# Shifting, norming and transposing a token-major residual stream in a six-layer attention and feed-forward kernel

## The reference, cut to what matters

```python
x = L0_attn_x                                  # (2, 1024, 128)
xn = layernorm(x)
s = recurrent_branch(xn)                       # projections, causal conv, gates, scan, projection
y = xn
for i in range(6):
    y = attn_layer(shift_tokens(y), Wqkv[i], q_scale[i], k_scale[i], Wo[i]) + y    # 16 heads of 64, window 32
    y = ffn_layer(shift_tokens(y), ln_g[i], ln_b[i], W1[i], b1[i], W2[i], b2[i]) + y
out = x + s * silu(y)

def shift_tokens(t):                           # the second half of the channels comes from the token before
    a, s = split(t, 2, -1)
    return concat([a, s moved one token down], -1)

def ffn_layer(x, g, bln, W1, b1, W2, b2):
    xn = (x - mean(x)) / sqrt(var(x) + 1e-5) * g + bln      # over the 128 channels
    a, gate = split(xn @ W1 + b1, 2, -1)                    # 341 columns each
    return a * gelu(gate) @ W2 + b2
```

## Time and profile before

| | |
|---|---|
| runs | 1633.87, 1634.21, 1636.32 us; median 1634.21 |
| span of the profiled execution | 1634.9 us |
| busy: PE, DVE, ACT, POOL | 1595.9, 1395.7, 1341.3, 1321.6 us |
| mean granted TensorE clock | 0.994 of full speed |
| chain that ended last | PE 87%, ACT 4%, POOL 2%, DVE 2%, issue 2% |

### The profile page before, as it was taken

How to read it: one execution, slowest core, us unless ns; L and a number is a source line. 1 busy time by engine, 2 the same in 40 slices (tenths; PEclk the granted TensorE clock), 3 DMA queues, 4 the chain that set the end, 5 groups by cost and what they waited for, 6 DMA issues and landing times.

```text
span 1634.9 us, 50862 instructions
## 1 busy us (share of the span) xinstructions
PE 1595.9 (98%) x19920; PEld 1370.2 (84%) x19920; DVE 1395.7 (85%) x2021; ACT 1341.3 (82%) x2516; POOL 1321.6 (81%) x1278
## 2 busy tenths in 40 slices
PE   5999999999999999999999999999999999999997
PEld 3778888888888888888888888888888888888886
DVE  7888888888888888888888888888888899999975
ACT  5778888888888888888888888888888888888874
POOL 9888899888889888889888889888888777777741
PEclk8999999999999999999999999999999999999999
DMA  5234233333323344232344324244332332222231
GB/s 166 80 114 138 73 95 93 113 109 100 106 75 93 102 117 121 75 108 70 96 112 127 99 73 111 70 121 109 110 95 76 85 101 73 78 73 70 64 90 58
DMA packets 184872, 156.89 MB, mean 96 GB/s; under 512 B 111551, under 2 KB 156093, under 8 KB 184637
## 3 DMA queue, kind: packets, MB, share of 16 engines
q1 hardware_dynamic: 184636, 153.64, 33.6%
HBM read 27.56 MB, written 1.05 MB: 17 GB/s over the span
## 4 chain that ended last, share of the span: by engine, by line
PE 87%; ACT 4%; POOL 2%; DVE 2%; issue 2%; DMA 0%; SPq 0%; ACTq 0%; POOLq 0%; DVEq 0%
PE ps_pv L807 12%; PE ps_s L783 11%; PE ps_pv L826 10%; PE ps_tr L744 9%; PE ps_qn L719 9%; PE ps_qn L720 7%; PE ps_qn L721 7%; PE ps_tr L731 5%; PE ps_pv L816 3%; PE ps_qn L906 2%; PE ps_qn L907 2%; PE ps_s L766 2%; PE ps_qn L908 2%; PE ps_qn L893 1%; PE ps_pv L864 1%
## 5 line engine op out<-in xcount | busy, mean ns | idle before, releaser
L2032 POOL TENSOR_TENSOR qk<-qk,t 128x1024 f32<-128x1024 f32 x192 | 456.0, 2376 | 82.0 <-DVE qk L1550 81.4
L1547 DVE TENSOR_TENSOR t<-ps_qn,tab 128x512 f32<-128x512 f32 x384 | 264.3, 688 | 121.5 <-ACT sq L1145 109.9
L2044 POOL TENSOR_TENSOR qkr<-qk,rinv 128x1024 f32<-128x1024 f32 x192 | 361.5, 1903 | 8.0 <-POOL rinv L2024 0.8
L1132 ACT ACTIVATE pbd<-ps_tr 64x512 f32<-64x512 f32 x384 | 226.4, 590 | 55.3 <-PE ps_tr L731 51.7
L719 PE MATMUL ps_qn<-w_hi,xs_hi 128*128 128x512 f32 x576 | 260.9, 453 | 10.8 <-DVE qk L1550 8.1
L1550 DVE TENSOR_TENSOR qk<-ps_qn,tab 128x512 f32<-128x512 f32 x384 | 260.9, 679 | 0.0
L1145 ACT ACTIVATE sq<-ps_qn 128x512 f32<-128x512 f32 x384 | 228.8, 596 | 32.7 <-PE ps_qn L721 27.9
L1178 ACT ACTIVATE qbd<-ps_tr 64x512 f32<-64x512 f32 x384 | 227.3, 592 | 34.2 <-PE ps_tr L744 28.7
L720 PE MATMUL ps_qn<-w_lo,xs_hi 128*128 128x512 f32 x576 | 229.8, 399 | 0.0
L721 PE MATMUL ps_qn<-w_hi,xs_lo 128*128 128x512 f32 x576 | 229.2, 398 | 0.0
L1560 DVE TENSOR_REDUCE ss<-sq 128x32 f32<-128x2048 f32 x96 | 216.5, 2256 | 0.0
(11 more groups left out here) (177 smaller groups left out, 3178.7 us busy)
## 6 DMA issues: line engine op xcount, KB each, us to landing
v_own<-v_new SPq DMA_DIRECT2D x96, 512.0 KB, 3.3
v_back<-v_new SPq DMA_DIRECT2D x96, 384.0 KB, 3.5
v_back<-v_own SPq DMA_DIRECT2D x94, 128.0 KB, 2.3
kT<-kT SPq DMA_DIRECT2D x84, 128.0 KB, 2.7
w_raw<-in_Wqkv SPq DMA_DIRECT2D x18, 512.0 KB, 5.0
rot<-in_rot SPq DMA_DIRECT2D x48, 128.0 KB, 2.7
fx<-xmid SPq DMA_DIRECT2D x96, 64.0 KB, 2.1
xsh<-x SPq DMA_DIRECT2D x190, 32.0 KB, 2.6
```

The costliest lines, as they stand in the source:

```text
L1547: v.tensor_tensor(t2[:, part].rearrange("p (h s d) -> p h s d", s=2, d=DH // 2), swapped, tab[:, 2 * k + 1:2 * k + 2, :].rearrange("p o (s ...
L2032: g.tensor_tensor(qk[b][:, part], qk[b][:, part], t2[:, part], ALU.add).then_inc(added[b], 1)
L2044: g.tensor_tensor(qkr[b][:, part].rearrange("p (h d) -> p h d", d=DH), qk[b][:, part].rearrange("p (h d) -> p h d", d=DH), rinv[b][:, k * ...
```

## The change

Both residual tiles now have the tokens of a tile on the partitions. Each row has 192 columns: the 128 channels stand in columns 64 to 191 (`OWN`), and columns 0 to 63 take the second half of the channels of the token before, so that columns 0 to 127 (`MIXED`) are the shifted row in another order of channels; the weights' rows are permuted on the host to match. `xmid` keeps four tiles.

- The shift becomes a DMA from partition to partition, in place, one for 127 partitions and one for the first.
- The norm's mean and variance come from VectorE's `bn_stats` and `bn_aggr` along the row; GpSimd subtracts and scales with two `tensor_scalar` into `normal`. The centring, variance and broadcast products and `diag`, `fc`, `fsq` go.
- TensorE transposes the shifted x of the next half step's tile, and in b=0 also the two normalised rows of `normal`, in a new fill of ps_tr called `("mixed", b)`. ScalarE empties it: twice for x (`xsh`, `xs_hi`), twice with gain and offset for the norm (`fxn_hi`, `fxn`).
- The output, down and branch projections swap the stationary and the moving side, so that tokens come out on the partitions; the down projection has 128 columns moving instead of 256, for each stream apart. b2 enters as a further row of W2 against a row of ones.
- At the end the result is token-major already, so the transposes of the result go. The normalised input is written into `x` by tokens, and its transposes go into `branch` alone.

```diff
 def tr_order(i):
     ...
-            order += [("qk", b, f) for f in (2, 3, 0, 1)]
+            order += [("qk", b, f) for f in (2, 3)]
+        if has_mixed(i, b):
+            order += [("mixed", b)]
+        if valid(i - 1):
+            order += [("qk", b, f) for f in (0, 1)]
     return order
+
+def has_mixed(i, b):
+    return valid(next_tile(i, b)[0]) or (b == 0 and valid(i - 4))
...
-        sp.dma_start(w.xsh[b][0:64, :], x[0:64, b, own]).then_inc(w.x_shifted[b], 16)
-        sp.dma_start(w.xsh[b][64:P, :], x[64:P, b, before]).then_inc(w.x_shifted[b], 16)
+        sp.dma_start(x[1:P, :, k, 0:HALF], x[0:P - 1, :, k, DIM:WIDE]).then_inc(w.x_shifted[k % 2], 16)
+        sp.dma_start(x[0:1, :, k, 0:HALF], before).then_inc(w.x_shifted[k % 2], 16)
...
+                def transpose_mixed(i, b):
+                    if not has_mixed(i, b):
+                        return
+                    bank, n = fill(tr_order, i, ("mixed", b))
+                    ring_free(pe, tr_done, bank, n)
+                    t, s = next_tile(i, b)
+                    if valid(t):
+                        pe.wait_ge(x_shifted[t.n % 2], 32 * (t.n // 2 + 1))
+                        last = tr(ps_tr[bank][:, 0:P], x[:, s, t.tile, MIXED], ident[:, :])
+                    if b == 0 and valid(i - 4):
+                        pe.wait_ge(normed, (i - 4).n + 1)
+                        for s in range(B):
+                            last = tr(ps_tr[bank][:, P + s * P:P + (s + 1) * P], normal[:, s, :], ident[:, :])
+                    last.then_inc(tr_full[bank], 1)
...
-                        last = mm(ps_pv[bank][:, DOWN], w2[0:w, c, :], hid[0:w, c, :, :].rearrange("p b t -> p (b t)"),
+                    for s in range(B):
...
+                            last = mm(ps_pv[bank][:, P + s * P:P + (s + 1) * P], hid[rows, c, s, :], w2[rows, c, :], start=(c == 0), stop=end)
...
-                        last = mm(ps_pv[bank][:, 0:P], wo[:, hp, :], oT[:, hp, :, :].rearrange("p a c -> p (a c)"),
+                        last = mm(ps_pv[bank][:, 0:P], oT[:, hp, :, :, :].rearrange("p u a q -> p (u a q)"), wo[:, hp, :],
...
                         ffn_down(i)
                         transpose_keys(i, b)
-                        ffn_centre(i)
+                        transpose_mixed(i, b)
                         rec_hidden(i, b)
                         out_projection(i, b)
...
                         transpose_keys(i, b)
+                        transpose_mixed(i, b)
...
                         qkv(i, b, (4, 5))
-                        ffn_broadcast(i)
                         ffn_up(i, 2)
...
+                def evac_mixed(i, b):
...
+                        f(xsh[s][:, :], ps_tr[bank][:, 0:P], ACT.Copy)
+                        last = f(xs_hi[s][:, :], ps_tr[bank][:, 0:P], ACT.Copy)
+                    if b == 0 and valid(m):
...
+                        for to in (fxn_hi, fxn):
+                            last = f(to[:, :, :].rearrange("p b t -> p (b t)"), ps_tr[bank][:, P:P + B * P], ACT.Identity,
+                                     bias=ln_gb[:, SM_B:SM_B + 1], scale=ln_gb[:, SM_G:SM_G + 1])
+                    last.then_inc(tr_done[bank], 1)
...
+                def mid_statistics(n):
+                    dve.wait_ge(fx_in, (n.n + 1) * 32)
+                    after_first(dve, normed, n.n, n)
+                    for s in range(B):
+                        v.bn_stats(mid_stats[:, s, :], mid(n, s, MIXED)).then_inc(mid_stat, 1)
+                    dve.wait_ge(mid_stat, 2 * B * n.n + B)
+                    for s in range(B):
+                        v.bn_aggr(mid_mv[:, s, :], mid_stats[:, s, :]).then_inc(mid_stat, 1)
+                    dve.wait_ge(mid_stat, 2 * B * (n.n + 1))
...
+                def normalise_mid(n):
+                    wait_fill(pool, tr_full, tr_order, n + 3, ("mixed", 0))
+                    for s in range(B):
+                        last = g.tensor_scalar(normal[:, s, :], mid(n, s, MIXED), mid_mv[:, s, 0:1], rinv[0][:, 2 * HEADS + s:2 * HEADS + s + 1],
+                                               ALU.subtract, ALU.mult)
+                    last.then_inc(normed, 1)
```

More of the change, by code:

```diff
@@ L519, in _, with shift_x @@
             def _(sp):
[L520 to L521 removed]
+                def shift_x(t):
+                    if not valid(t):
                         return
                     if t.n < TILES:
[L524 to L527 removed]
+                        sp.wait_ge(s_xn, 2 * t.n + 2)
+                    else:
+                        wait_fill(sp, pv_done, pv_order, t - 3, ("out", 0))
+                    if t.n > 1:
+                        wait_fill(sp, tr_full, tr_order, t - 2, ("mixed", 0))
+                    w.shift_x(sp, t)
                 def shift_xmid(i):
@@ L627, in half @@
                         shift_xmid(i)
-                    if b == (1 if i.first else 0):
+                    late = i.n == 1
+                    if b == (1 if i.first else 0) and not late:
                         load_rotary(i)
-                    late = (i.n, b) == (1, 1)
-                    if not late:
-                        shift_x(*next_tile(i, b))
+                    if b == 0 and not late:
+                        if i.first:
+                            shift_x(i)
+                        shift_x(i + 1)
                     carry_k(i, b)
@@ L825, in project_out @@
                     for hp in range(HP):
-                        last = mm(ps_pv[bank][:, 0:P], wo[:, hp, :], oT[:, hp, :, :].rearrange("p a c -> p (a c)"),
+                        last = mm(ps_pv[bank][:, 0:P], oT[:, hp, :, :, :].rearrange("p u a q -> p (u a q)"), wo[:, hp, :],
                                   start=(hp == 0), stop=(hp == HP - 1))
-                    return last
-                def variance(i, bank):
-                    wait_fill(pe, qn_done, qn_order, i, "centre")
-                    for s in range(B):
-                        last = mm(ps_pv[bank][:, VAR + s:VAR + s + 1], fsq[:, s, :], mean_col[:, :], start=True, stop=True)
                     return last
@@ L845, in out_projection @@
                 def out_projection(i, b):
-                    j, n = i - 2, i - 3
-                    if not valid(j):
+                    if not valid(i - 2):
                         return
                     bank = next_pv_bank(i, ("out", b))
-                    last = project_out(i, b, bank)
-                    if b == 0 and valid(n):
-                        last = variance(i, bank)
-                    if b == 0 or not valid(n):
-                        last.then_inc(pv_full[bank], 1)
-                def ffn_broadcast(i):
-                    n = i - 3
-                    if not valid(n):
-                        return
-                    bank, k = fill(pv_order, i, spread_of(i))
-                    if i.n >= STEPS:
-                        ring_free(pe, pv_done, bank, k)
-                    pe.wait_ge(diag_ready, n.n + 1)
-                    mm(ps_pv[bank][:, DOWN], ones[:, :], flat(diag), start=True, stop=True).then_inc(pv_full[bank], 1)
+                    project_out(i, b, bank).then_inc(pv_full[bank], 1)
                 def last_out(i, b):
@@ L1391, in half @@
                     evac_k(i, b, 1)
[L1392 to L1397 removed]
+                    evac_mixed(i, b)
                     rec_tanh(i, b)
```

533 lines of the change are left out of this document (210 added, 323 removed).

## The result

The changed kernel takes 1854.75 us (median of four runs, 1848.1 to 1857.58), the kernel before 1635.05 in the same comparison: a ratio of 1.134, with a 95% interval of 1.1316 to 1.1362. The prediction said 1681, between 1655 and 1700. The direction was right, and four fifths of the loss were not in the sum.

The account below looks back on a forecast made before the run. TensorE's own instruction stream was taken to bound the kernel. +1.17 us a step over 36 steps (+42), +5 for seven later steps, +3 for the first four and -4 after the last gave +46 on 1634.9: 1681 us, range 1655 to 1700.

Parts of the forecast that it names:

- the part on other places: Whether ScalarE's, VectorE's, GpSimd's and SyncE's changed work delays TensorE anywhere else: all costed at 0.
- The ring wait: Mixed transposes behind the key fills wait for ScalarE's first kT copy: 0.57 us in b=0, 0.90 in b=1.
- TensorE's work: Work per half step: -0.41 us in b=0, +0.11 in b=1 for one new transpose.
- The broadcast: Its removal (L864) in b=1 was taken as 0 us, since it fills an existing wait; bounds 0 and 0.43.
- Rival A: No added wait, ScalarE's copies being over in time, so only work counts: about 1612 us; chance 0.09.
- Rival B, the falling clock: New stalls make TensorE's clock fall once a step: +1.55 us over 45 steps, 1751 us; chance 0.05.
- The Trainium skill's rule on small idles: Small idles between groups cycling through PSUM banks make the clock swing; by it the time is the falling clock's 1751.
- The tail: After the last step, products go for nine transposes and the chain shortens: -4 us, bounds 0 and -8.
- VectorE's statistics: In b=0 two statistics and two aggregates, some 1 us before the v copies: price 0, cover 0.6.
- GpSimd's two operations: They replace diag with half its columns each, in the half step before TensorE reads them: cost 0.
- the down projection: In b=0, 12 passes of 128 columns for 6 of 256: 1.34 us for 1.29, +0.05.
- the start and the first four steps: Start 0, give or take 3 us; first four steps between 0 and 6, taken as 3.

Follow-up runs that it names:

- all three edits: Changed kernel with the key copy first on SyncE, 127 rows cut in 112 and 15, and mixed transposes moved: 1652.57 us, ratio 1.0108.

## Why the prediction missed

**The step that failed** stands in the part on other places: "SyncE issues two DMAs for x where it issued four, and both row shifts land half a step or more before their reader. All this I cost at 0." Both halves of the sentence are right, and neither is the question. I counted issues and asked when the shifts are read. I never asked what they cost the queue they stand in, nor who stands behind them. The key copy does. It had 1.4 us to spare in the kernel before, and the earlier trace rows had it as ScalarE's last release once already (0.7 us), which the argument passed over. The change issued it 4.6 us later in its queue, it landed 3.9 us later, and ScalarE waited 3.0 us for it in 39 half steps. A shift by offset takes 0.6 us a DMA on the queue; nothing in the rows bounded what a DMA of 127 rows and one of one row would take there. Issuing the key copy ahead of the shifts takes the time from 1854.75 to 1700.92: 154 of the 174 us by which the forecast was short.

**The ring wait** had the right mechanism and place; its size was a little off. With the key copy first, a step grew by 0.88 us instead of 1.17: b=1 by 0.83 for 1.01, b=0 by 0.06 for 0.16. From the end of the keys to the mixed fill it was 0.87 in b=1 (1.66 less 0.79, forecast 0.90) and 0.47 in b=0 (1.35 less 0.88, forecast 0.57). Moving the fill took back 0.57 and 0.44 of it.

**TensorE's work.** Without waits the b=0 half step is 15.23 to 15.25 for 15.63, so -0.38 to -0.40; the sum said -0.41. In b=1 it is +0.26 to +0.28 where it said +0.11. The broadcast was indeed not won: from the fifth qkv chunk to the third up chunk it is 1.73 us in both kernels (813.81 to 815.54 before, 609.29 to 611.02 with the key copy first). In the broadcast's place the third up chunk's weight loads wait for VectorE's v_new, 24.1 us in 39 waits between 60 and 1560 us of the changed kernel; the kernel before has 0.3 us in one. The excess stands at the moved fill: the first two up chunks with the transpose of x between them take 1.78 us (683.82 to 685.60 with all three edits) for 1.50 (811.47 to 812.97), so 0.28 for a transpose that I costed at 0.11. Rival A's steps (-0.30 and more) are thus not reached even without a wait: -0.13.

**Rival B, the falling clock.** I gave it 0.05 on stalls of 0.6 and 0.9 us, and with those the clock did stay (0.990 with the key copy first). It fell in 22 of the 33 middle steps behind stalls of 2.3 to 3.5 us, and cost 1.67 us each time; my price was 1.55. That is some 37 us of the 152 in these steps. It came on top of the failed step, not in place of the forecast. The Trainium skill's rule on small idles between groups that cycle through banks (cited in the prediction) is not what the runs show here: the kernel with ring waits of 0.3 and 0.6 us keeps 0.990, the one with waits of about 3 us has 0.963.

**The tail** was forecast at -4 and is +17 with the key copy first (66.0 us behind the last scores for 49.0). I took the work that goes and a chain that becomes shorter, and the chain became longer. The shift lands 5.6 us after its first issue with 127 rows (1666.46 to VectorE's start at 1672.07), and 3.3 with 112 and 15 (1624.80 to 1628.11). GpSimd's last probabilities were put behind a rest that waits for the mixed transposes. This term had the wrong sign, is off by 21 us and is, with the half steps in which v_new came late, the reason for 1701 instead of 1681. Both are offset in part by the smaller step.

**The rest** came out as costed: VectorE's statistics (0.49, 0.25 us a step) and GpSimd's two operations (0.80 each, 1.6 a step, for 0.62 of the `diag` that I took as equal) delay nobody in the middle; the down projection takes 1.34 (932.22 to 933.56), as worked out; the start and the first four steps are +3.1 for +3.

## What to carry to other kernels

When a change replaces transfers, price each new DMA as an occupant of its queue, and name what is issued behind it and who waits for that; "it lands in time" answers only for its own reader. A transfer of 127 rows in two pieces each was cheap to issue here (0.71 us) and dear for the next one (2.8 us): put what is urgent ahead of it, or cut it in 112 and 15. Where a wait of an engine is listed with a small total, as the 0.7 us for the key copy, work out how much its releaser has to spare (1.4 us here) and what queues behind it when it comes later than that; a stall of about 3 us can cost the clock besides.

## What the hardware showed unexpectedly

- A DMA of 127 rows with two pieces of 256 B each took 0.71 us on SyncE's queue and made the next one take 2.6 to 3.0 (4.4 once in each of the two kernels), whichever it was. Behind 112 rows the next took 0.96, behind 15 rows 0.68. Behind 127 rows of one piece of 512 B it took 0.97, although that transfer too used about one engine's worth (share 0.07); what makes the hold is thus open.
- After stalls of TensorE of 2.3 to 3.5 us with busy work before and behind, the granted clock went to 0.50 for about 3 us in 22 of 33 cases, and in 33 of 33 after stalls of 3.0 to 4.0 us (one-row DMA first). With stalls up to 1.7 us (mixed transposes later) it fell in none of the 33.
- With the same lateness of one DMA (118.6 us of ScalarE's waits) the run took 1855 or 1757 us. In the first TensorE met it in one stall of about 2.8 us, in the second behind the output projection in two, 0.9 and 0.8 in the mean. The clock, which no longer fell, is the largest part of the difference (some 37 us); some 20 are the b=1 waits of 0.6 us, which went too.
